# A GRU, two attentions and a mixture of experts on one core: gate inputs formed inside the GRU loop, weights loaded a stage ahead, a filter stage in overlapping batches

## The chip, the cores and the metric

One NeuronCore of a Trainium2 chip runs the whole program, in float32. The metric is the device time of one execution in microseconds (us); lower is better.

## The reference

x has 4 batches of 512 tokens of 512 features. The cut reference:

```python
for t in range(512):                       # GRU over the tokens, h starts as cond
    gi = x[:, t] @ W_ih + b_ih;  gh = h @ W_hh + b_hh
    r = sigmoid(gi_r + gh_r);  z = sigmoid(gi_z + gh_z)
    n = tanh(gi_n + r * gh_n);  h = (1 - z) * n + z * h
a = differential_attention(hs)             # 16 heads, causal and reversed, rotary, lambda
a = filter_over_tokens(a)                  # a fixed 512x512 circulant matrix
x1 = x + head_rms_norm(a) * w @ Wout
xn = rms_norm(x1) * (1 + scale(cond)) + shift(cond)
y = full_attention(xn) @ W_out
out = x1 + y + moe(y)                      # 64 experts, top 6, plus a shared expert
```

Each GRU step needs the h of the step ahead. The gate inputs gi need only x.

## The kernel before, in words

The program is a row of stages, each a function with one block per engine (PE, ACT, DVE, POOL, and SP for DMA), with semaphores between the engines and a barrier at its end. Each engine runs its instructions in the order in which they are written. Weights for the next stage are loaded into one buffer, `ahead`, where that is free.

`gate_inputs_stage` (L55) turns x into `xT` with PE transposes, spreads W_ih into `wih`, forms the r and n gate inputs of all 512 tokens (`gates`, L110 to L125: 4 batches, 8 tiles of 128 gate columns, 4 matmuls each of 512 tokens), moves them with bias into `giT` (L142 on ACT, L144 on DVE), and forms the z inputs as rows in `giz` (L132).

`gru_stage` (L195) loads W_hh on three queues (`load`, L234), then runs 512 steps. One step on PE: `add_z_input` (L292, waits for `pick_ready`, since a small matrix `pick` selects the step's row out of `zin`), `add_bias` (L287), then three gates of 16 matmuls (`gate`, L300) into PSUM tiles pr, pn and pz. The first gate waits for `h_ready`, in halves of h. DVE transposes the rows, ACT forms the sigmoids and tanh, and two DVE scans per step make h, one for each half (`HALVES`, L228, L393); then DVE copies h into `hsT`, which lies in the tile `wide` (L400). POOL copies a block of 32 steps of z inputs into `zin` (L275) and then one `pick` for each step (L280), two buffers deep. The PE and DVE loops hold two steps for each round.

`diff_attention_stage` (L408) follows, loading h and weights per group through SP. `filter_stage` starts with SP loads of filt, wout, wemb, and small vectors, among them a transposed load of cond (L1030), forms scale and shift with 64 matmuls (L1048), and then runs a loop over 4 batches, each in a straight line: filter matmuls (L1055), squares on ACT, head norms on DVE (L1131 to L1140), transposes (L1062), Wout matmuls (L1068), residual and norm, transposes (L1074), xnT. `full_attention_stage`, `route_stage` and `expert_stage` each load their first weights once they have begun; `combine_stage` gathers the expert outputs.

Of the kernel before, what the change touches and what calls it, by code (L numbers as in the profile page):

```python
# [54 lines left out]
def gate_inputs_stage(nc, t, x, W_ih, b_ih, b_hh):  # L55


    with ExitStack() as ctx:
        sem = ctx.enter_context(Sems(nc, "gi_"))
        wih = ctx.enter_context(nc.sbuf_tensor("wih", [P, KD, G3], F32))  # L60
        wraw = t.ahead[:, 0:2 * G3].rearrange("p (a n) -> p a n", a=2)
        xin = ctx.enter_context(nc.sbuf_tensor("gi_xin", [P, 2, TT, D], F32))
        xT = t.wide[:].rearrange("p (b k t) -> p b k t", b=B, k=KD)
        bias = ctx.enter_context(nc.sbuf_tensor("gi_bias", [P, 2, GC], F32))
# [13 lines left out]
        @block.sync  # L78
        def _(sp):
            sp.dma_start(t.ident[:], t.const["ident"]).then_inc(ident_in, 16)  # L80
            for b in range(B):
                if b >= 2:
                    sp.wait_ge(xT_psum, (b - 1) * KD)
                sp.dma_start(xin[:, b % 2, :, :], x[b, :, :].rearrange("(tt p) d -> p tt d", p=P)).then_inc(x_in[b % 2], 16)
            for n, bvec in enumerate((b_ih, b_hh)):
                sp.dma_start(zbias[:, n, :], bvec[D:2 * D].unsqueeze(0).broadcast_to([P, D])).then_inc(zb_in, 16)

        @block.gpsimd
        def _(pool):
            for k in range(KD):  # L90
                if k >= 2:
                    pool.wait_ge(w_spread, 3 * (k - 1))
                pool.dma_start(wraw[:, k % 2, :], W_ih[k * P:(k + 1) * P, :]).then_inc(w_in[k % 2], 16)

        @block.tensor
        def _(pe):
            pe.wait_ge(ident_in, 16)
            for b in range(B):
                pe.wait_ge(x_in[b % 2], 16 * (b // 2 + 1))
                for k in range(KD):  # L100
                    n = b * KD + k
                    if n >= 2:
                        pe.wait_ge(xT_ready, n - 1)
                    for tt in range(TT):
                        last = nc.tensor.transpose(pt[:, k % 2, tt * P:(tt + 1) * P], xin[:, b % 2, tt, k * P:(k + 1) * P], t.ident[:])
                    last.then_inc(xT_psum, 1)
            pe.wait_ge(w_spread, 3 * KD)
            pe.wait_ge(xT_ready, B * KD)

            def gates(b):  # L110
                for c in range(NG):

                    if c >= 4:
                        pe.wait_ge(gi_even if c % 2 == 0 else gi_odd, b * (NG // 2) + (c - 4) // 2 + 1)
                    col = GATES[c // KD] * D + (c % KD) * P
                    for k in range(KD):
                        last = nc.tensor.matmul(pg[:, c % 4, :], wih[:, k, col:col + P],
                                                xT[:, bass.ds(b, 1), k, :].rearrange("p o t -> p (o t)"),
                                                start=(k == 0), stop=(k == KD - 1))
                    last.then_inc(gi_psum, 1)  # L120

                pe.wait_ge(gi_even, b * (NG // 2) + NG // 2)
                pe.wait_ge(gi_odd, b * (NG // 2) + NG // 2)

            with pe.Fori(0, B) as b:  # L125
                gates(b)
            for kb in range(T // 32):
                if kb >= 4:
                    pe.wait_ge(z_out, kb - 3)
                for k in range(KD):  # L130
                    for b in range(B):
                        last = nc.tensor.matmul(pg[32 * b:32 * b + 32, kb % 4, :], xT[:, b, k, 32 * kb:32 * kb + 32], wih[:, k, D:2 * D],  # L132
                                                start=(k == 0), stop=(k == KD - 1))
                last.then_inc(z_psum, 1)

        def evict(eng, b, c, out_sem):

            eng.wait_ge(gi_psum, b * NG + c + 1)
            dst = t.giT[:, :, bass.ds(b + c * B, 1)].rearrange("p t o -> p (t o)")
            g = GATES[c // KD] * KD + c % KD  # L140
            if c % 2 == 0:
                nc.scalar.activation(dst, pg[:, c % 4, :], ACT.Identity, bias=bias[:, 0, g:g + 1]).then_inc(out_sem, 1)  # L142
            else:
                nc.vector.tensor_scalar(dst, pg[:, c % 4, :], bias[:, 0, g:g + 1], None, ALU.add).then_inc(out_sem, 1)  # L144

        @block.scalar
        def _(act):
            for n, bvec in enumerate((b_ih, b_hh)):
                for j in range(KD):
                    for g in GATES:  # L150
                        act.dma_start(bias[32 * j:32 * j + 32, n, g * KD:(g + 1) * KD],
# [3 lines left out]
            with act.Fori(0, B) as b:  # L155
                for c in range(0, NG, 2):
                    evict(act, b, c, gi_even)

# [1970 lines left out]
```

## Time and profile before

| what | us |
|---|---|
| median of 3 runs | 4526.82 (4515.19 to 4535.55) |
| the profiled execution | 4517.86 |
| its span | 4516.1 |
| PE busy | 3734.1 (83%) |
| DVE busy | 2242.8 (50%) |
| ACT busy | 1318.2 (29%) |
| POOL busy | 527.0 (12%) |
| mean granted TensorE clock | 0.945 |

The busy times are shares of the span of one profiled execution. PE is TensorE, PEld its weight loads, which overlap. A float32 matmul appears as two records. A granted clock of 1.00 is 2.4 GHz and 0.50 is 1.2 GHz. A line number such as L305 is a line of the kernel above.

### The profile page before, as it was taken

To read this page: it belongs to the slowest core of one execution; us is meant where nothing else is said; L and a number is where in the kernel's file an instruction comes from. 1 tells how busy PE (TensorE), PEld (TensorE's weight loads), DVE (VectorE), ACT (ScalarE), POOL (GpSimd) and SP (SyncE) were. 2 spreads that over 40 slices of the span, in tenths; PEclk is the share of its full clock that TensorE was granted. 3 is DMA by queue.
4 is the path that set the end of the run, shared out by engine and by line. 5 is a ranking of instruction groups with operands and counts; after the bars stand their busy time and mean duration, and the time that the engine had idled before them with its cause. 6 is when DMAs were issued, how large, how long until landed. Compare 5 with 4: busy or idle time off the path is not lost. (4 is left out here: it accounts for less than half of the span.)

```text
span 4516.1 us, 167227 instructions
## 1 busy us (share of the span) xinstructions
PE 3734.1 (83%) x68303; PEld 2458.8 (54%) x68364; DVE 2242.8 (50%) x6299; ACT 1318.2 (29%) x4238; POOL 527.0 (12%) x1085
## 2 busy tenths in 40 slices
PE   7888888888888888887899998477999979688850
PEld 3277777777777777776444443243333334344420
DVE  2155555555555555554677777133666643222224
ACT  1023333333333333332344444122444411011100
POOL 0000000000000000000222232000000004300026
PEclk9999999999999999999999999688999979899975
DMA  2150000000000000001111110201111111288769
GB/s 70 29 177 0 0 0 0 0 0 0 0 0 0 0 0 0 0 0 39 42 42 49 49 33 17 81 25 50 49 65 49 49 65 57 74 261 261 261 181 202
DMA packets 144489, 256.71 MB, mean 57 GB/s; under 512 B 25943, under 2 KB 76247, under 8 KB 142388
## 3 DMA queue, kind: packets, MB, share of 16 engines
q1 hardware_dynamic: 102004, 159.95, 10.8%
q0 software_dynamic: 21248, 53.30, 4.4%
q10 hardware_dynamic: 21184, 42.76, 3.1%
q8 instruction: 33, 0.54, 0.1%
q14 instruction: 20, 0.16, 0.0%
HBM read 147.89 MB, written 62.92 MB: 47 GB/s over the span
## 5 line engine op out<-in xcount | busy, mean ns | idle before, releaser
L305 PE MATMUL gru_pr<-gru_whh,h 128*4 128x128 f32 x16384 | 543.7, 273 | 230.6 <-DVE h L396 230.6
L305 PEld LDWEIGHTS gru_pr<-gru_whh,h 128*4 128x4 f32 x16384 | 388.4, 87 | 373.9 <-DVE h L396 367.8
L305 PE MATMUL gru_pz<-gru_whh,h 128*4 128x128 f32 x16384 | 541.3, 273 | 1.3 <-issue 1.3
L305 PE MATMUL gru_pn<-gru_whh,h 128*32 128x128 f32 x16384 | 541.7, 273 | 0.0
L305 PEld LDWEIGHTS gru_pn<-gru_whh,h 128*32 128x32 f32 x16384 | 458.4, 110 | 1.3
L305 PEld LDWEIGHTS gru_pz<-gru_whh,h 128*4 128x4 f32 x16384 | 438.3, 87 | 9.3 <-issue 1.4
L376 DVE STREAM_TRANSPOSE gru_tr<-gru_pr 128x128 f32<-128x128 f32 x512 | 162.3, 317 | 380.0 <-PE gru_pr L305 380.0
L340 ACT ACTIVATE gru_rn<-gru_pre 128x16 f32<-128x16 f32 x512 | 118.4, 231 | 700.4 <-DVE gru_pre L378 700.4
L280 POOL COPY gru_pick<-ident 128x4 f32 x512 | 96.5, 188 | 1685.2 <-PE gru_pz L296 1679.9
L891 DVE TENSOR_REDUCE da_mx<-da_ps 128x2 f32<-128x1024 f32 (+3 forms) x256 | 201.2, 817 | 133.5 <-PE da_ps L582 133.5
L389 DVE STREAM_TRANSPOSE gru_tz<-gru_pz 128x64 f32<-128x64 f32 x1024 | 194.6, 229 | 120.2 <-PE gru_pz L305 120.2
L798 ACT ACTIVATE da_probT<-da_ps 128x1024 f32<-128x1024 f32 (+3 forms) x256 | 169.5, 701 | 196.1 <-PE da_ps L603 196.1
L396 DVE TENSOR_TENSOR_SCAN h<-gru_d 128x32 f32<-128x32 f32 x1024 | 185.7, 223 | 78.3 <-ACT gru_d L345 77.8
L296 PE MATMUL gru_pz<-gru_zin,gru_pick 128*4 128x128 f32 x4096 | 205.9, 273 | 19.4 <-DMA gru_whh<-in_L_cond_W_hh 19.4
L380 DVE STREAM_TRANSPOSE gru_tn<-gru_pn 128x128 f32<-128x128 f32 x512 | 162.2, 317 | 119.6 <-PE gru_pn L305 119.6
L342 ACT ACTIVATE gru_d<-gru_narg 128x32 f32<-128x32 f32 x512 | 120.6, 236 | 329.6 <-DVE gru_narg L385 329.6
L345 ACT ACTIVATE gru_d<-gru_tz 128x8 f32<-128x8 f32 x1024 | 176.9, 216 | 128.0 <-DVE gru_tz L389 128.0
L1674 POOL DMA_INDIRECT xg<-ro_yb,ro_slot x96 | 94.4, 983 | 991.7 <-issue 918.5
L290 PE MATMUL gru_pn<-gru_bias,gru_one 128*32 128x128 f32 x4096 | 205.9, 273 | 0.0
L509 POOL TENSOR_SCALAR_AFFINE_SELECT da_probT<-da_probT 128x256 f32<-128x256 f32 x256 | 142.8, 569 | 420.9 <-ACT da_probT L798 420.8
L1864 PE MATMUL ex_pg<-ex_wg,ex_xT 128*128 128x384 f32 x512 | 189.4, 516 | 0.0
L1455 DVE TENSOR_REDUCE fa_mx<-fa_ps 128x2 f32<-128x1024 f32 x128 | 150.5, 1217 | 51.7 <-PE fa_ps L1275 51.6
(266 smaller groups left out, 5457.4 us busy)
## 6 DMA issues: line engine op xcount, KB each, us to landing
ex_wg<-in_L_ffn_gate_up_proj SPq DMA_DIRECT2D x64, 768.0 KB, 4.7
ex_wd<-in_L_ffn_down_proj ACTq DMA_DIRECT2D x64, 384.0 KB, 6.7
xg<-gru_zeros SPq DMA_DIRECT2D x4, 4096.0 KB
da_hb<-wide SPq DMA_DIRECT2D x16, 1024.0 KB, 4.7
fa_hb<-xnT SPq DMA_DIRECT2D x16, 1024.0 KB
ex_xg<-xg ACTq DMA_DIRECT2D x64, 256.0 KB, 6.0
eo<-ex_eo POOLq DMA_DIRECT2D x64, 256.0 KB, 5.4
da_wg<-ahead SPq DMA_DIRECT2D x48, 256.0 KB, 4.9
```

The source lines that it names most:

```text
L290: nc.tensor.matmul(pn[32 * j:32 * j + 32, 0:P], one[:], bias[:, j, :], start=True, stop=False)
L296: last = nc.tensor.matmul(pz[32 * j:32 * j + B, par, 0:P], pick[:, par, :], zin[:, j * P:(j + 1) * P], start=True, stop=False)
L305: last = nc.tensor.matmul(rows(j), of(c), whh[:, c, g, j, :], start=(c == 0 and start), stop=(c == KD - 1))
L345: nc.scalar.activation(cb(d1[:, half * HS:(half + 1) * HS, 2]), tz[:, half * HC:(half + 1) * HC, 0:B], ACT.Sigmoid).then_inc(z_act, 1)
L376: nc.vector.transpose(tr[:].rearrange("p c x -> p (c x)"), pr[:, 0:P]).then_inc(tr_done, 1)
L380: nc.vector.transpose(tn[:], pn[:, 0:P]).then_inc(tn_done, 1)
L389: nc.vector.transpose(tz[:, half * HC:(half + 1) * HC, :].rearrange("p c x -> p (c x)"), pz[:, par, half * 64:(half + 1) * 64]).then_inc(t ...
L396: nc.vector.tensor_tensor_scan(t.h[:].rearrange("p c x -> p (c x)")[:, half * 64:(half + 1) * 64:2], d0[:, of, :].rearrange("p c o -> p (c ...
L798: nc.scalar.activation(probT[:, n % 2, 2 * part:2 * part + 2, n * P:T], ps[:, KBANK[2 * part]:KBANK[2 * part] + 2, n * P:T], ACT.Exp, scal ...
L891: nc.vector.tensor_reduce(mx[:, i, a, 2 * part:2 * part + 2], ps[:, bank:bank + 2, 0:(i + 1) * P], AX, ALU.max).then_inc(max_done, 1)
L1455: nc.vector.tensor_reduce(mx[:, i, 2 * half:2 * half + 2], ps[:, 2 * half:2 * half + 2, :], AX, ALU.max).then_inc(max_done, 1)
L1864: last = nc.tensor.matmul(pg[:, u % 2, 0:2 * I], xT[:, u % 2, k, :], wg[:, u, k, :], start=(k == 0), stop=(k == KD - 1))
```

## The change

1. **Gate inputs.** `gate_inputs_stage` forms the r and n inputs of the first 32 steps only. The others are formed inside the GRU loop, for the block of 32 steps ahead: 8 tiles c, of 4 matmuls k each, one matmul in each step (`next_gate_input`). POOL copies the weights of tile c to a fixed place `wst`, because the loop variable c selects them; DVE moves the finished tile into `giT` after every fourth step (`move_gate_input`). The PE, DVE and POOL loops become 15 blocks of 8 groups of 4 steps, and a last block of 32 steps without gate inputs.
2. **GRU tail.** The two parts of h are one chunk and three (`PARTS`), where they were two and two.
3. **Weights a stage ahead.** A second buffer `ahead2`. W_hh and cond are loaded in the gate input stage, filt in the first attention, the first route weights at the end of the second attention, the gate_up weights of the first 4 experts at the end of the route stage.
4. **Filter.** cond and the small vectors are loaded as rows and turned on PE; scale and shift come from 8 wide matmuls; the batches are unrolled and overlap: PE applies the filter of batch i, then turns y of i - 1 and xn of i - 2, then multiplies by Wout for i - 1.

The core of the diff (semaphore declarations, renamed tiles and the body of DVE's step left out):

```diff
@@ gate_inputs_stage @@
-            with pe.Fori(0, B) as b:
-                gates(b)
+            for c in range(NG):
+                if c >= 2:
+                    pe.wait_ge(gi_out, c - 1)
+                for k in range(KD):
+                    last = nc.tensor.matmul(pg[:, c % 2, 0:B * 32], wih[:, k, c * P:(c + 1) * P], xT[:, k, :, 0:32], start=(k == 0), stop=(k == KD - 1))
+                last.then_inc(gi_psum, 1)
...
+            sp.wait_ge(w_spread, 3 * KD)
+            whh = t.ahead[:].rearrange("p (c g j f) -> p c g j f", c=KD, g=3, j=KD)
+            for jj in range(KD):
+                rows = W_hh.rearrange("(jj c i) n -> jj i c n", jj=KD, c=KD)[jj]
+                for c in range(KD):
+                    sp.dma_start(whh[32 * jj:32 * jj + 32, c, :, :, :].rearrange("i g j f -> i (g j f)"), rows[:, c, :]).then_inc(whh_in, 16)
@@ gru_stage @@
-        HALVES = (0, 1)
-        HC, HS = KD // 2, ST // 2
+        PARTS = (slice(0, 1), slice(1, KD))
...
+            with pool.Fori(0, NBL - 1) as kb:
+                block_of_z(kb)
+                with pool.Fori(0, NG) as c:
+                    pool.wait_ge(gi_out, kb * NG + c + 1)
+                    nc.gpsimd.tensor_copy(wst[:], wih[:, :, bass.ds(c * P, P)]).then_inc(wst_ready, 1)
+                    for k in range(KD):
+                        pick_step(kb, c * KD + k, k)
...
-                    if s is not None and c % HC == 0:
-                        pe.wait_ge(h_ready, s * 2 + (c // HC + 1))
+                    if s is not None and c < 2:
+                        pe.wait_ge(h_ready, s * 2 + (c + 1))
...
-            with pe.Fori(0, T // 2) as q:
+            def next_gate_input(kb, c, k):
+                if k == 0:
+                    pe.wait_ge(gi_out, kb * NG + c + 1)
+                    pe.wait_ge(wst_ready, kb * NG + c + 1)
+                last = nc.tensor.matmul(pgi[:, 0:P], wst[:, k, :], xT[:, k, :, bass.ds(kb * 32 + 32, 32)],
+                                        start=(k == 0), stop=(k == KD - 1))
+                if k == KD - 1:
+                    last.then_inc(gi_psum, 1)
+
+            with pe.Fori(0, NBL - 1) as kb:
+                with pe.Fori(0, NG) as c:
+                    for k in range(KD):
+                        s = kb * 32 + c * KD + k
+                        add_z_input(s, k % 2)
+                        add_bias(s)
+                        next_gate_input(kb, c, k)
+                        step(s, k % 2)
...
+            def move_gate_input(kb, c):
+                dve.wait_ge(gi_psum, kb * NG + c + 1)
+                nc.vector.tensor_tensor(t.giT[:, bass.ds(kb * 32 + 32, 32), bass.ds(c * B, B)], pgi[:, 0:P].rearrange("p (b t) -> p t b", b=B),
+                                        t.gi_bias[:, 0, bass.ds(c, 1)].unsqueeze(2).broadcast_to([P, 32, B]), ALU.add).then_inc(gi_out, 1)
+
+            with dve.Fori(0, NBL - 1) as kb:
+                with dve.Fori(0, NG) as c:
+                    for k in range(KD):
+                        if k == 0:
+                            dve.wait_ge(gi_out, kb * NG + 1)
+                        step(kb * 32 + c * KD + k, k % 2)
+                    move_gate_input(kb, c)
@@ diff_attention_stage, before its first loads of h @@
+            sp.dma_start(t.filt[:], t.const["filt"].rearrange("(s p) t -> p s t", p=P)).then_inc(filt_in, 16)
@@ filter_stage, PE after its first two batches' filters @@
+            for i in range(2, B + 1):
+                if i < B:
+                    apply_filter(i)
+                turn(y[:, (i - 1) % 2, :, :], y_ready, i - 1)
+                moved = tuple(used)
+                turn(xn, normed, i - 2)
+                times_wout(i - 1, moved)
+            turn(xn, normed, B - 1)
@@ full_attention_stage, after its last loads @@
+            sp.dma_start(t.ro_wout, w_out.rearrange("(k p) n -> p k n", p=P)).then_inc(ahead_in, 16)
+            sp.dma_start(t.ro_stage[0:E, 0, :], gate_w).then_inc(ahead_in, 16)
+            sp.dma_start(t.ro_stage[:, 1:4, :], sg_w.rearrange("(c p) n -> p c n", p=P)).then_inc(ahead_in, 16)
@@ route_stage, after its last load @@
+            for u in range(t.EU):
+                sp.dma_start(t.ex_wg[:, u, :, :], gate_up[u].rearrange("(p k) i -> p k i", p=P)).then_inc(S["wg_in"], 16)
```

DVE sets gi_out to 1 ahead of its loop, so the first group waits for nothing.

The order of the instructions at three places of the GRU loop follows. Semaphores are used again by later stages and are printed under the name of their first use: gi_x_in1 stands for gi_out here, gi_xT_ready for z_added, gi_whh_in for zin_ready, gi_w_in0 for wst_ready, gi_xT_psum for pick_ready, gi_x_in0 for the loop's gi_psum, gi_z_out for tn_done, and gi_ident_in for h_ready. A DVE scan is printed as SCALAR_TENSOR_TENSOR. In the kernel before, the same names gi_xT_ready and gi_bias_ready stand for zin_ready and z_added. ISA and REGISTER_ALU rows are waits and address work.

POOL in the block loop of the kernel before, from the copy of a block of z inputs to the end of the loop over steps:

```order
L275 COPY gru_zin<-giz 128x512
L276 UNCONDITIONAL_BRANCH
L276 ISA
L279 ISA [waits gi_xT_ready]
L280 ISA [waits gi_bias_ready]
L280 COPY gru_pick<-ident 128x4
L279 REGISTER_ALU [waits gi_xT_ready]
L280 ISA [waits gi_bias_ready]
L280 COPY gru_pick<-ident 128x4
L276 REGISTER_ALU
L276 COMPARE_AND_BRANCH
```

The same place in the changed kernel, up to the second of a group's four picks:

```order
L262 COPY gru_zin<-giz 128x512
L271 UNCONDITIONAL_BRANCH
L271 ISA
L273 ISA [waits gi_x_in1]
L273 COPY gru_wst<-ahead 128x512
L265 REGISTER_ALU
L266 ISA [waits gi_whh_in]
L267 ISA [waits gi_xT_ready]
L267 COPY gru_pick<-ident 128x4
L266 ISA [waits gi_whh_in]
L267 ISA [waits gi_xT_ready]
L267 COPY gru_pick<-ident 128x4
```

A copy of 128x512 with a wait for gi_out now stands ahead of each group's first pick.

DVE in the changed kernel, from the scans of the fourth step of a group to the end of the inner loop:

```order
L407 SCALAR_TENSOR_TENSOR h<-gru_d 128x16 [waits gru_z_act]
L405 REGISTER_ALU
L407 SCALAR_TENSOR_TENSOR h<-gru_d 128x48 [waits gru_z_act]
L410 REGISTER_ALU
L411 ISA [waits gi_ident_in]
L411 COPY wide<-h 128x16
L414 ISA
L415 ISA [waits gi_x_in0]
L415 TENSOR_TENSOR giT<-gru_pgi,gi_bias 128x32x4
L419 REGISTER_ALU
```

The move of a tile into giT stands behind the scans and the copy of h of the fourth step.

PE in the changed kernel, from the top of a group of four steps to its first gates:

```order
L292 ISA [waits gi_xT_psum]
L294 MATMUL gru_pz<-gru_zin,gru_pick 4x128 [waits gru_tz_done]
L294 MATMUL gru_pz<-gru_zin,gru_pick 4x128 x3
L288 MATMUL gru_pn<-gru_bias,gru_one 32x128 [waits gi_z_out]
L288 MATMUL gru_pn<-gru_bias,gru_one 32x128 x3
L315 ISA
L317 ISA [waits gi_w_in0,gi_x_in1]
L317 MATMUL gru_pgi<-wide,gru_wst 128x128
L301 REGISTER_ALU
L303 MATMUL gru_pr<-ahead,h 4x128 [waits gi_ident_in]
```

The matmul for the block ahead, with its waits in the first step of a group, stands between the bias and the gru_pr gate, which it didn't do before.

## Rows read from the trace of the kernel before

**Rows 1.** Busy time by stretch: length, PE, PEld, DVE, ACT, POOL, clock, DMA, GB/s
```profile
32.00:152.00 120.00, 112.84 (x260) 49.14 (x264) 17.80 (x17) 23.43 (x20) 0.00 (x0) 0.98 0.00 0
152.00:207.00 55.00, 55.00 (x512) 17.55 (x507) 10.38 (x15) 0.00 (x0) 0.00 (x0) 1.00 0.01 1
207.00:226.40 19.40, 0.00 (x1) 0.00 (x1) 3.83 (x14) 1.53 (x3) 3.45 (x8) 0.57 0.83 163
226.40:2122.40 1896.00, 1663.04 (x57344) 1498.29 (x57344) 1038.27 (x4607) 595.03 (x3071) 105.28 (x525) 1.00 0.03 11
...
2836.50:2891.70 55.20, 13.81 (x64) 13.72 (x64) 0.72 (x4) 1.30 (x2) 0.00 (x0) 0.50 0.47 157
2891.70:3084.40 192.70, 148.31 (x384) 74.78 (x384) 65.39 (x124) 39.33 (x104) 0.00 (x0) 0.85 0.05 16
...
3922.80:4366.00 443.20, 352.29 (x1152) 195.97 (x1152) 87.98 (x192) 60.71 (x129) 34.80 (x64) 0.94 0.76 246
```
**Rows 2.** Timeline of one GRU step: start, length, engine, line, [idle before <-releaser]
```profile
1000.53 1.06 PE L305 MATMUL gru_pz<-gru_whh,h 128*4 128x128 f32 x32
...
1001.40 0.40 PE L296 MATMUL gru_pz<-gru_zin,gru_pick 128*4 128x128 f32 x8
...
1001.62 0.40 PE L290 MATMUL gru_pn<-gru_bias,gru_one 128*32 128x128 f32 x8
1001.65 0.38 DVE L389 STREAM_TRANSPOSE gru_tz<-gru_pz 128x64 f32<-128x64 f32 x2 [0.23 <-PE gru_pz L305]
...
1002.00 0.19 POOL L280 COPY gru_pick<-ident 128x4 f32 x1 [3.50 <-PE gru_pz L296]
1002.19 0.36 DVE L396 TENSOR_TENSOR_SCAN h<-gru_d 128x32 f32<-128x32 f32 x2 [0.15 <-ACT gru_d L345]
...
1002.47 1.06 PE L305 MATMUL gru_pr<-gru_whh,h 128*4 128x128 f32 x32 [0.44 <-DVE h L396]
...
1002.67 0.18 DVE L400 COPY wide<-h 128x16 f32 x1
...
1003.34 1.06 PE L305 MATMUL gru_pn<-gru_whh,h 128*32 128x128 f32 x32
```
**Rows 3.** Timeline of POOL at the start of a block of 32 steps
```profile
344.03 0.61 POOL L275 COPY gru_zin<-giz 128x512 f32 x1 [7.19 <-PE gru_pz L296]
344.94 0.41 POOL L280 COPY gru_pick<-ident 128x4 f32 x2 [0.30 <-POOL gru_zin L275]
```
**Rows 4.** Groups of instructions: busy us, mean ns of one, idle before and releaser
```profile
L563 PE MATMUL da_ps<-da_wg,da_hb 128*128 128x128 f32 x512 | 65.3, 281 | 0.0
...
L144 DVE TENSOR_SCALAR giT<-gi_pg,gi_bias 128x512 f32 x16 | 17.5, 1093 | 101.7 <-PE gi_pg L117 101.7
L192 DVE TENSOR_TENSOR giz<-gi_pg,gi_zbias 128x512 f32<-128x512 f32 x16 | 11.1, 692 | 45.2 <-PE gi_pg L132 45.2
```
**Rows 5.** Stretches of the expert stage: length, PE busy, clock, DMA, GB/s
```profile
3992.35:3994.77 2.42, 0.00 (x1) 1.00 0.60 157
3994.77:3998.77 4.00, 4.00 (x11) 0.57 0.97 338
3959.38:3962.04 2.66, 0.00 (x1) 1.00 0.72 203
3962.04:3966.04 4.00, 4.00 (x16) 1.00 0.88 306
```
**Rows 6.** Timeline of PE in the first two GRU steps
```profile
227.21 1.93 PE L305 MATMUL gru_pr<-gru_whh,h 128*4 128x128 f32 x32
...
230.42 1.05 PE L305 MATMUL gru_pz<-gru_whh,h 128*4 128x128 f32 x32
...
236.08 0.62 PE L305 MATMUL gru_pz<-gru_whh,h 128*4 128x128 f32 x15 [1.26 <-issue]
```
**Rows 7.** Timeline at the entry of the filter stage
```profile
2839.84 29.97 SPq L1030 DMA_DIRECT2D fi_condT<-in_cond  x4
...
2876.94 13.81 PE L1048 MATMUL fi_pf<-fi_condT,fi_wemb 128*128 128x4 f32 x64 [41.06 <-DMA fi_bg<-in_L_cond_g_norm]
```
**Rows 8.** Timeline at the entry of the route stage
```profile
3662.76 0.69 PE L1577 MATMUL ro_pa<-ident,ro_stage 64*128 64x64 f32 x4 [16.11 <-DMA ro_sdraw<-in_L_ffn_shared_down_w]
```

More of the change, by code:

```diff
@@ L97, in _ @@
             pe.wait_ge(ident_in, 16)
             for b in range(B):
-                pe.wait_ge(x_in[b % 2], 16 * (b // 2 + 1))
                 for k in range(KD):
[L101 to L106, printed above, removed]
+                    transpose_x(b, k)
@@ L1044, in _, with bank @@
         def _(pe):
[L1045 to L1052 removed]
+            used = [0, 0]
+            def bank(v):
+                if used[v]:
+                    pe.wait_ge(dve_moved if v else act_moved, used[v])
+                used[v] += 1
+                return pt[:, v, :]
@@ new lines, in _ @@
+            pe.wait_ge(cond_ready, 2)
+            to = bank(1)
+            for k in range(KD):
+                for n in range(2):
+                    last = nc.tensor.matmul(to[32 * n:32 * n + B, :], condT[:, k, :], wemb[:, k, n * D:(n + 1) * D],
+                                            start=(k == 0), stop=(k == KD - 1))
+            last.then_inc(turned, 1)
+            turn(y[:, 0, :, :], y_ready, 0)
+            moved = tuple(used)
+            pe.wait_ge(emb_ready, 2)
+            to = bank(1)
@@ new lines, in _ @@
+            for k in range(KD):
+                last = nc.tensor.transpose(to[:, k * NR:(k + 1) * NR], embr[:, k * P:(k + 1) * P], t.ident[0:NR, 0:NR])
+            last.then_inc(turned, 1)
+            pe.wait_ge(wout_in, 16)
+            times_wout(0, moved)
+            for i in range(2, B + 1):
+                if i < B:
+                    apply_filter(i)
+                turn(y[:, (i - 1) % 2, :, :], y_ready, i - 1)
+                moved = tuple(used)
+                turn(xn, normed, i - 2)
+                times_wout(i - 1, moved)
@@ new lines, in _ @@
+            dve.wait_ge(cond_ready, 2)
+            dve.sem_inc(dve_moved, 1)
+            norm_heads(1)
+            dve.wait_ge(turned, 2)
+            dve.wait_ge(embr_zero, 1)
+            for n in range(2):
+                nc.vector.tensor_copy(embr[32 * n:32 * n + B, :], pt[32 * n:32 * n + B, 1, :]).then_inc(emb_ready, 1)
+            dve.wait_ge(emb_ready, 2)
+            dve.sem_inc(dve_moved, 1)
+            seen[0] += 2
+            keep_y(0)
+            seen[0] += 1
+            dve.wait_ge(turned, seen[0])
@@ L1521, in _, with route_stage @@
             output(NIT - 1)
-def route_stage(nc, t, W_out, gate_w, sg_w, su_w, sd_w):
+def route_stage(nc, t, su_w, sd_w, gate_up):
     with ExitStack() as ctx:
```

533 lines of the change are left out of this document (284 added, 249 removed).

## The prediction

> **What bounds the kernel now.** I read the busy times by stretch first, then the timeline of one GRU step, then the same step's neighbours on POOL, then the places where the change touches other stages. The stretches [rows 1] show that 1,896 of the 4,516 us are the 512 GRU steps, at a TensorE clock of 1.00 (2.4 GHz), 3.70 us each. Inside a step PE idles 0.44 us ahead of the gru_pr gate, released by DVE's scan that makes h [rows 2]: the loop is a recurrence PE, DVE, ACT, DVE, PE, and whatever is put between that scan and the next gru_pr gate lengthens it. What PE does in the gap (z input from 1001.40, bias from 1001.62, so 0.22 us of issue) is hidden. Ahead of the loop lie 120 us of gate inputs, 55 us of z inputs and 19.4 us of waiting for W_hh [rows 1]. The filter stage waits 55 us at its entry, and its own 192.7 us hold only 148.3 us of PE at a clock of 0.85 [rows 1].
>
> **The change part by part**, summed against the profiled execution (4517.9 us; the median of the runs shown, 4526.8, is 9 us above it). About 0.5%, 23 us, is what a measurement of this kernel can tell from no change.
>
> (a) Gate inputs ahead of the GRU. Removed from the stage: 256 records of 0.43 us of issue, the 120 us. Left: block 0 only, 8 tiles x 4 matmuls, two records each, at 0.128 us a record (65.3 us / 512 for 128x128 in [rows 4]), 8 us, plus a cold start, 9 us. The 55 us of z inputs stay. Gain 111. W_hh is now loaded under the z inputs; of the 19.4 us there remain DVE's memsets (3.8 us busy in [rows 1]) and one small load, 5.5 us. Gain 14. Together **-125**. The order of the x and W_ih loads differs, but the bytes are the same: bounds -115 and -130.
>
> (b) Filter stage. Its entry wait of 41 us is for small loads, among them the transposed cond load that SP takes 30 us to issue, and 13.8 us of matmuls follow [rows 7]. Both go: the filter is preloaded, and these matmuls become 8 wide ones between batches: 54 us. The body: PE's 148.3 us at 0.85 are 126 at full clock, plus 5 for the cond work. Of 44 us of idle time I keep about 25: the last head norms and the last root still stand ahead of a turned batch in about five places, some 4 us each, with a tail at the end. That is 156 in place of 193. Together **-91**, bounds -75 and -100.
>
> (c) Route stage: its first matmul comes at 3662.76, after 16.1 us of idle time for loads [rows 8]. W_out, gate_w and sg_w are now there; sd_w and su_w (1.5 MB) are still waited for a little later: **-8**, bounds 0 and -11. (d) Expert stage: it runs at 246 GB/s with DMA busy 0.76 [rows 1], so 3 MB of weights fetched earlier are worth 3 / 0.246 = 12 us: **-11**, bounds 0 and -14. (e) The attention stage's first h load now stands behind the 1 MB filter load on SP's queue, 4 us at that rate: **+3**, bounds 0 and +5.
>
> (f) Uneven tail. Two transposes take 0.38 us, two scans 0.36, and the first scan's end releases PE 0.06 us later [rows 2]. A first part of one chunk frees PE up to 0.08 us sooner, but after 4 matmuls (0.22 us) PE waits for the second part, whose transpose and scan are now three chunks long. They end about when the second halves did. I take 0.01 us a step, **-5**; bounds -40 (0.08 x 512) and +10.
>
> (g) What the GRU loop gains. Per step one matmul, 0.26 us, and its address work go into the 0.44 us gap: nothing in three steps of four; if it didn't fit, 0.1 us x 360 = 36 us, which the range holds. The fourth is another matter. In the order of DVE, move_gate_input stands behind the whole fourth step. Its signal gi_out releases two things: POOL's copy of the next weights (wst), which stands ahead of the four picks on POOL, and PE's first matmul of the next group. PE's z input of step 4c+4 needs the first pick. So once in four steps this chain lies between the scan and gru_pr. From the end of the second scan (1002.19 + 0.36 = 1002.55) by the rows: the h copy ends at +0.30 (1002.67 + 0.18) [rows 2]. The move is 128 elements out of PSUM into giT. Of 512 elements such an operation takes 0.69 us, into strided giT 1.09 [rows 4], so it lies between 0.17 and 0.55; I take 0.35, nearer a quarter plus fixed cost, and 0.05 of dispatch: +0.70. POOL starts 0.20 after its release (1001.80 to 1002.00 [rows 2]); the wst copy has the size of the zin copy, 0.61 us, and after that one the pick started 0.30 later where it waited for it; picks in a row follow each other by about 0.22 [rows 3]. Pick done at +1.75 (to 2.0). PE starts z at +1.85, then 0.22, 0.22, 0.26 for the gate input and 0.15 for waits and addresses: gru_pr at +2.70. Now it starts at -0.08. The stall is **2.8 us**, bounds 2.2 and 3.5. It occurs for c = 1 to 7 of 15 blocks and for c = 0 of 14: 119 times, **+333**, bounds +262 and +417.
>
> (h) The clock. In this stall PE idles from the end of gru_pz (1000.53 + 1.06, or -0.96) to +1.85, 2.8 us. No GRU step shows such a gap. The nearest rows are in the expert stage: after 2.42 us of idle the clock was 0.57 over the next 4 us, after 2.66 us it stayed at 1.00 [rows 5]; of the eight gaps of 1.9 to 2.7 us at full clock in this trace (these are two) six were followed by a fall to 1.2 GHz, for some 3.4 us. The price of cold gates: the first step of all, after 19 us of idle, took 3.21 us for its first two gates (227.21 to 230.42), where a warm gate takes 0.87 (1002.47 to 1003.34), so 1.5 us a fall [rows 2, 6]. With a fall in three of four stalls: 1.1 us, **+131**. Bounds 0 (it never falls) and 3 us a stall, +357 (two such stretches).
>
> Sum: 4517.9 - 125 - 91 - 8 - 11 + 3 - 5 + 333 + 131 = 4746; with the 9 us of the median, **4755 us**, 5% slower.
>
> **The rivals.** (1) *Faster.* The gains are 237 us; the hand-over decides at 237 / 119 = 1.99 us. If DVE's move, POOL's copy and the picks overlap more than the rows show (a copy of 0.3 us, a pick right behind it) and the clock holds, a stall of 1.7 us gives 4526.8 - 237 + 202 = 4492. For it: waits that are long satisfied cost little here. Against: four operations on three engines in strict order, each with a row. 0.07. (2) *No difference,* the same with 1.9 to 2.1 us: 0.03. (3) *The clock holds*: 4755 - 131 = 4624. For it: two gaps of eight; GRU steps keep 1.00 with their own short gaps. 0.22. (4) *The clock falls long*: another 1.8 us a stall, 4755 + 214 = 4969. For it: the filter stage, with 44 us of gaps in 193, ran at a mean clock of 0.85 [rows 1]. 0.13. (5) *Code loading.* PE's loop body doubles to four steps. At the second step ever, PE stood 1.26 us for nothing but issue [rows 6]. Were that paid each time round the longer body, 120 x 1.26 = 151 us more: 4906. Against: it is not paid again in the two-step loop, where each gap ends with DVE. 0.05. The Trainium skill (Runtime: NRT & Kernel Launch, "Instruction fetch mechanics") says that a taken branch whose target is outside the window held forces a fetch and a stall, while it gives PE room for 2048 instructions. Some 230 matmuls of four instructions each would be inside that, by that page; no run here shows the count.
>
> **How the numbers follow.** The forecast has 0.50, the rivals 0.50. The range reaches from rival 3 with a stall of 2.6 us (4624 - 24 = 4600) to just under rival 4, **4600 to 4950**; that leaves out rivals 1 and 2 and half of rival 4. Faster 0.07, within 0.5% 0.03, slower 0.90.
>
> **What would show it.** In the profile after: the GRU loop begins near 102 us and takes about 2,355 us. On POOL one 0.6 us copy in every four steps, released by DVE's move into giT; PE's z matmul then waits for POOL's pick, 119 times about 2.8 us. The granted clock of the loop is about 0.90. The filter stage takes about 157 us with no entry wait, the experts about 432. The forecast is wrong if PE's waits for the pick are under 1 us, or if the loop's clock is 1.00; if the GRU loop still takes under 2,130 us, the change wins.

## The result, and the profile of the changed kernel

| | before | changed |
|---|---|---|
| median of 4 runs | 4525.65 us | 4800.05 us |
| lowest and highest | 4515.19, 4535.55 | 4775.56, 4810.63 |
| span of the profiled execution | 4516.1 us | 4809.0 us |
| mean granted clock | 0.945 | 0.921 |

The ratio is 1.060, with a 95% interval of 1.055 to 1.065. The change makes the kernel 6% slower, against 5% (4755 us) forecast.

I read the stretches first, cut where TensorE (PE) starts and ends a stage. Busy time by stretch, changed kernel (columns as in [rows 1]):

```profile
33.70:42.30 8.60, 7.65 (x68) 7.37 (x72) 0.56 (x1) 3.74 (x8) 0.00 (x0) 1.00 1.03 211
42.30:97.40 55.10, 55.06 (x512) 16.46 (x512) 10.36 (x15) 0.37 (x1) 0.00 (x0) 1.00 0.02 4
97.40:103.90 6.50, 0.04 (x4) 0.05 (x8) 3.83 (x14) 1.62 (x3) 1.95 (x5) 0.83 0.44 164
103.90:2491.30 2387.40, 2029.11 (x58304) 1691.51 (x58304) 1113.99 (x4723) 612.72 (x3068) 163.60 (x644) 0.92 0.02 8
2491.30:3209.00 717.70, 647.42 (x5011) 286.27 (x5068) 492.80 (x639) 322.94 (x516) 183.54 (x288) 0.96 0.14 44
3209.00:3389.20 180.20, 143.28 (x410) 70.03 (x409) 66.17 (x124) 40.56 (x106) 0.00 (x0) 0.89 0.17 60
...
3954.40:4218.10 263.70, 215.02 (x704) 108.51 (x704) 96.27 (x229) 32.22 (x78) 94.09 (x96) 0.94 0.18 63
4218.10:4648.60 430.50, 360.78 (x1152) 202.78 (x1152) 87.96 (x192) 60.02 (x128) 34.11 (x63) 0.92 0.77 245
```

Ahead of the GRU the plan works: the gate inputs take 8.6 us, not 120, the wait for W_hh has become 6.5 us, and the first GRU matmul starts at 103.9 us, not 226.4. The loop behind it loses four times as much. Its 2,387.4 us, at a clock of 0.92, stand against the 1,894.9 us, at 1.00, that the same cut gives for the kernel before:

```profile
226.40:2121.30 1894.90, 1663.02 (x57344) 1498.29 (x57344) 1037.53 (x4603) 594.57 (x3069) 105.28 (x525) 1.00 0.03 11
2835.90:3081.90 246.00, 162.08 (x448) 88.50 (x448) 65.30 (x127) 41.11 (x106) 0.00 (x0) 0.78 0.14 48
3646.70:3922.80 276.10, 216.99 (x704) 109.42 (x704) 96.75 (x229) 32.23 (x78) 94.40 (x96) 0.91 0.16 55
3922.80:4357.00 434.20, 352.28 (x1152) 195.97 (x1152) 87.98 (x192) 60.11 (x128) 34.25 (x63) 0.94 0.77 250
```

What PE waits for in the changed kernel's loop says which term it is. Waits of PE from 103.9 to 2491.3 us (line, releaser: us in total, times, longest):

```profile
PE gru_pz L294 <- POOL gru_pick L267: 342.0, 120, 6.5
PE gru_pr L303 <- DVE h L407: 14.0, 46, 0.4
PE gru_pz L303 <- issue: 4.7, 2, 3.5
PE gru_pn L288 <- issue: 4.0, 1, 4.0
```

The first row is 6.5 us ahead of the loop and 119 waits of 2.82 us in it. The wait for DVE's scan, which the matmul of the next gate input now fills, is all but gone. One hand-over, once in four steps, in the timeline of the changed kernel:

```profile
1010.36 1.06 PE L303 MATMUL gru_pz<-ahead,h 128*4 128x128 f32 x32
...
1011.98 0.44 DVE L407 TENSOR_TENSOR_SCAN h<-gru_d 128x16 f32<-128x16 f32 x2
1012.54 0.18 DVE L411 COPY wide<-h 128x16 f32 x1
1012.90 0.29 DVE L415 TENSOR_TENSOR giT<-gru_pgi,gi_bias 128x128 f32 x1 [0.17 <-issue]
1013.36 0.61 POOL L273 COPY gru_wst<-ahead 128x512 f32 x1 [4.85 <-DVE giT L415]
...
1013.91 0.32 POOL L267 COPY gru_pick<-ident 128x4 f32 x2
1014.24 0.40 PE L294 MATMUL gru_pz<-gru_zin,gru_pick 128*4 128x128 f32 x8 [2.82 <-POOL gru_pick L267]
1014.45 0.40 PE L288 MATMUL gru_pn<-gru_bias,gru_one 128*32 128x128 f32 x8
1014.79 0.49 PE L317 MATMUL gru_pgi<-wide,gru_wst 128*128 x2
...
1015.20 1.06 PE L303 MATMUL gru_pr<-ahead,h 128*4 128x128 f32 x32
```

The scans end at 1012.42, gru_pr starts 2.78 us later. What is to be seen is a file of five operations on three engines, one behind the other: DVE's h copy, DVE's move, POOL's copy, POOL's pick, PE's z input.

What that wait does to the clock stands in the four hand-overs that follow one another here, each with the same wait of 2.82 us. First PE's timeline, then the busy time of the 4 us behind each:

```profile
1014.24 0.40 PE L294 MATMUL gru_pz<-gru_zin,gru_pick 128*4 128x128 f32 x8 [2.82 <-POOL gru_pick L267]
...
1031.76 0.40 PE L294 MATMUL gru_pz<-gru_zin,gru_pick 128*4 128x128 f32 x8 [2.82 <-POOL gru_pick L267]
...
1068.46 0.61 PE L294 MATMUL gru_pz<-gru_zin,gru_pick 128*4 128x128 f32 x8 [2.82 <-POOL gru_pick L267]
...
1088.80 0.61 PE L294 MATMUL gru_pz<-gru_zin,gru_pick 128*4 128x128 f32 x8 [2.82 <-POOL gru_pick L267]
```

```profile
1014.24:1018.24 4.00, 4.00 (x130) 3.58 (x130) 1.26 (x6) 0.47 (x2) 0.19 (x1) 1.00 0.00 0
1031.76:1035.76 4.00, 4.00 (x130) 3.58 (x130) 1.26 (x6) 0.47 (x2) 0.19 (x1) 1.00 0.00 0
1049.28:1053.28 4.00, 4.00 (x82) 3.49 (x86) 0.49 (x2) 0.23 (x1) 0.19 (x1) 0.67 0.00 0
1068.46:1072.46 4.00, 4.00 (x62) 2.79 (x66) 0.32 (x1) 0.00 (x0) 0.19 (x1) 0.50 0.00 0
```

In the same 4 us PE gets through 130 records at 2.4 GHz and 62 at 1.2 GHz. From hand-over to hand-over a group takes 17.5 us with the clock held (1014.24 to 1031.76), 19.2 with a short fall (1049.28 to 1068.46), and 20.3 to 20.8 with a long one (1068.46 to 1088.80). Over the loop's 118 groups, 57 hold the clock and 61 do not. It is no accident of the run: one pattern repeats every 16 groups, 8 held and 8 fallen (three short, five long).

### The profile page after: what moved, and what is told of

Its sections match the earlier page's. It is cut to its first block and busy times, and to the rows that moved or that the text cites. A ratio compares the mean times of both kernels' runs of the same rounds, so it can differ in the third digit from the quotient of the medians.

```text
span 4809.0 us, 169712 instructions
## 1 busy us (share of the span) xinstructions
PE 3982.5 (83%) x69032; PEld 2596.8 (54%) x69093; DVE 2302.2 (48%) x6400; ACT 1316.6 (27%) x4227; POOL 584.6 (12%) x1201
## 5 line engine op out<-in xcount | busy, mean ns | idle before, releaser
L303 PE MATMUL gru_pr<-ahead,h 128*4 128x128 f32 x16384 | 600.6, 289 | 14.0 <-DVE h L407 14.0
L303 PE MATMUL gru_pn<-ahead,h 128*32 128x128 f32 x16384 | 597.5, 291 | 0.0
L303 PE MATMUL gru_pz<-ahead,h 128*4 128x128 f32 x16384 | 572.5, 283 | 4.7 <-issue 4.7
L303 PEld LDWEIGHTS gru_pn<-ahead,h 128*32 128x32 f32 x16384 | 503.3, 118 | 10.6
L303 PEld LDWEIGHTS gru_pz<-ahead,h 128*4 128x4 f32 x16384 | 455.9, 91 | 33.5 <-issue 5.3
L303 PEld LDWEIGHTS gru_pr<-ahead,h 128*4 128x4 f32 x16384 | 366.3, 91 | 164.9 <-DVE h L407 29.8
L400 DVE STREAM_TRANSPOSE gru_tz<-gru_pz 128x32 f32<-128x32 f32 (+1 forms) x1024 | 194.8, 228 | 151.7 <-PE gru_pz L303 151.7
L407 DVE TENSOR_TENSOR_SCAN h<-gru_d 128x16 f32<-128x16 f32 (+1 forms) x1024 | 226.8, 229 | 57.3
L317 PE MATMUL gru_pgi<-wide,gru_wst 128*128 x960 | 247.3, 341 | 0.0
L354 ACT ACTIVATE gru_d<-gru_tz 128x4 f32<-128x4 f32 (+1 forms) x1024 | 198.3, 216 | 142.8 <-DVE gru_tz L400 142.8
```

Of the source, the lines that this page charges most:

```text
L303: last = nc.tensor.matmul(rows(j), of(c), whh[:, c, g, j, :], start=(c == 0 and start), stop=(c == KD - 1))
L317: last = nc.tensor.matmul(pgi[:, 0:P], wst[:, k, :], xT[:, k, :, bass.ds(kb * 32 + 32, 32)], start=(k == 0), stop=(k == KD - 1))
L354: nc.scalar.activation(cb(d1[:, part.start * B:part.stop * B, 2]), tz[:, part, 0:B], ACT.Sigmoid).then_inc(z_act, 1)
L400: nc.vector.transpose(tz[:, part, :].rearrange("p c x -> p (c x)"), pz[:, par, part.start * 32:part.stop * 32]).then_inc(tz_done, 1)
L407: nc.vector.tensor_tensor_scan(t.h[:].rearrange("p c x -> p (c x)")[:, part.start * 32:part.stop * 32:2], d0[:, of, :].rearrange("p c o -> ...
```

## The experiments

Four questions were open: whether the wait is the order of the work or the work itself (e1); what of the loss is the wait and what the clock (e4); how the wait divides (e2, e3); and why the small terms came out as they did (e5 to e9). e1 to e4 ran on one chip, e5 and e6 on a second, e7 to e9 on a third; the kernel before took 4517.9, 4541.7 and 4527.4 us there, so kernels on different chips are compared by their ratio to it. e2, e3 and e4 rest on two runs each, the others on four to six.

### e1: DVE's move one step earlier

```diff
                     for k in range(KD):
                         if k == 0:
                             dve.wait_ge(gi_out, kb * NG + 1)
+                        if k == KD - 1:
+                            move_gate_input(kb, c)
                         step(kb * 32 + c * KD + k, k % 2)
-                    move_gate_input(kb, c)
```

> The changed kernel with one call moved: DVE's move of the gate inputs stands ahead of the fourth step of a group, where DVE waits 0.65 us for the gru_pr gate, and no longer behind it. Theory (the stall is the order of DVE's move): the move, POOL's copy of 0.61 us and the picks all come a step earlier, PE never waits for a pick, the granted clock of the loop is 1.00, a group of four steps takes 4 x 3.64 = 14.6 us in place of 17.5 (clock held) or 20.4 (clock fallen), the GRU loop 1,870 us in place of 2,387, the kernel about 4,295 us (4,280 to 4,320), 5% under the kernel before. Rival (the longer loop body, loaded code, or the added matmul itself costs): a group stays over 15.5 us and the kernel over 4,400 us with an issue gap in each group. Rival (POOL is the bound: a copy of 0.61 us does not fit into a step): PE still waits for the pick, about 0.6 us a group, 4,370 us.

Measured: 4301.7 us, 0.953 of the kernel before (0.951 to 0.955), and 498 us under the changed kernel (483 by the two ratios). PE's waits from 110 to 1900 us hold no row of POOL's pick. A group in its timeline:

```profile
1005.05 0.19 DVE L411 COPY wide<-h 128x16 f32 x1
1005.40 0.29 DVE L415 TENSOR_TENSOR giT<-gru_pgi,gi_bias 128x128 f32 x1 [0.17 <-issue]
...
1005.86 0.61 POOL L273 COPY gru_wst<-ahead 128x512 f32 x1 [8.63 <-DVE giT L415]
...
1006.41 0.32 POOL L267 COPY gru_pick<-ident 128x4 f32 x2
...
1007.39 0.40 PE L294 MATMUL gru_pz<-gru_zin,gru_pick 128*4 128x128 f32 x8
```

The same instructions with the same durations: the move stands where DVE would wait for gru_pr anyway, POOL has its picks ready by 1006.73, and PE asks for one at 1007.39. The steps follow each other by 3.64 us and the clock of the loop is 1.00. So these 480 to 500 us are the place of one instruction in DVE's order. The rival of a longer loop body falls: PE has three issue gaps of over 1 us in the loop, 9.0 us in all; two lie in its first 20 us and one at the last block's own loop, and none comes again.

### e4: the wait kept, PE busy in it

```diff
                         s = kb * 32 + c * KD + k
+                        if k == 0:
+                            for _ in range(3):
+                                nc.tensor.matmul(spare[:], whh[:, 0, 0, 0, :], bias[:].rearrange("p j f -> p (j f)"), start=True, stop=True)
                         add_z_input(s, k % 2)
```

> The changed kernel with three matmuls of 128x512 that compute nothing (into a PSUM bank that nobody reads) ahead of the wait for the first pick of a group; they take 3 x 0.86 = 2.6 of the 2.8 us in which PE idles. Theory (two costs: the stall, and the falls of the clock that the idle time brings): the stall stays, the clock of the loop is 1.00, every group takes 17.5 us (57 of 118 do now, the others 19.2 to 20.8), the loop loses 118 x 1.31 = 155 us, and the kernel takes about 4,645 us. Rival (the clock falls for another reason, such as the matmuls' own load): no change, 4,800 us, or slower. Rival (the filler delays the z input): a group takes over 17.8 us.

Measured: 4651.5 us, 1.031 of the kernel before (1.028 to 1.033), 149 us less than the changed kernel (133 by the ratios) for 360 useless matmuls more: three ahead of each of the 120 groups, 119 of which have the wait. Timeline of PE, then the loop's busy time:

```profile
1011.71 2.84 PE L329 MATMUL gru_spare<-gru_bias,ahead 128*128 128x512 f32 x6
...
1014.60 0.40 PE L295 MATMUL gru_pz<-gru_zin,gru_pick 128*4 128x128 f32 x8
...
1015.15 0.49 PE L318 MATMUL gru_pgi<-wide,gru_wst 128*128 x2
```

```profile
103.10:2339.00 2235.90, 2207.60 (x59024) 1731.01 (x59024) 1116.50 (x4731) 614.14 (x3070) 163.80 (x647) 1.00 0.03 9
```

The clock is 1.00 and the next filler starts at 1029.22, 17.5 us after this one. This parts the two costs: the loops of changed kernel and e4 differ by 2387.4 - 2235.9 = 151.5 us, which is the clock; e4's and e7's (1888.7, below) by 347.2 us, which is the wait, 2.92 us each of 119 times. e4's stretch begins with its first filler, 4.4 us ahead of its first z input, so each of the two is known to about 5 us; a plain group of 17.51 us in e4 against 14.55 in e7 gives 2.96.

### e2 and e3: how the wait divides

e2 puts the first pick ahead of POOL's copy:

```diff
+                    pick_step(kb, c * KD, 0)
                     pool.wait_ge(gi_out, kb * NG + c + 1)
                     nc.gpsimd.tensor_copy(wst[:], wih[:, :, bass.ds(c * P, P)]).then_inc(wst_ready, 1)
-                    for k in range(KD):
-                        pick_step(kb, c * KD + k, k)
+                    for k in range(1, KD):
+                        pick_step(kb, c * KD + k, k % 2)
```

e3 lets POOL copy the next weights when PE has read the last ones, not when DVE has moved their result (gi_psum starts one higher there, and its other waits are one higher with it):

```diff
-                    pool.wait_ge(gi_out, kb * NG + c + 1)
+                    pool.wait_ge(gi_psum, kb * NG + c + 1)
                     nc.gpsimd.tensor_copy(wst[:], wih[:, :, bass.ds(c * P, P)]).then_inc(wst_ready, 1)
```

> The changed kernel with the first pick of a group ahead of POOL's copy of the weights; DVE's move stays where it is. Theory (a chain of DVE's move, POOL's copy, PE's matmul): z input and bias are issued in their normal place, PE's gate input matmul waits for the copy, which ends 0.94 + 0.61 us after the scan; gru_pr starts at +2.0 in place of +2.8, so a group at full clock takes 16.7 us in place of 17.5. PE idles some 1.9 us in place of 2.8. If the clock falls as often, the kernel takes about 4,705 us; if it holds, 4,550. Rival (the pick and z input are the stall): the wait vanishes, a group takes 14.6 us, 4,300 us.

> The changed kernel with POOL's copy of the weights released by PE's last matmul of the tile and no longer by DVE's move. Theory: copy and picks lie a step ahead, and only DVE's move (end at +0.77 us after the scan) stands between the scan and PE's gate input matmul, then 0.26 us for it: gru_pr at about +1.2 us, a stall of 1.3 us, a group of 15.9 us; PE's longest idle time is 1.2 us, and the clock holds at 1.00. Loop 2,030 us, kernel about 4,450 us; 4,530 with as many falls of the clock at half the price. Rival (POOL's 0.61 us copy is nothing, DVE's move is the whole stall): still 17.5 us a group, 4,800 us.

Measured: e2 4594.2 us, ratio 1.018 (1.015 to 1.021); e3 4483.4 us, ratio 0.993 (0.991 to 0.996). The loops' busy time and PE's longest wait in them, e2 and then e3:

```profile
103.90:2281.80 2177.90, 1878.63 (x58304) 1609.26 (x58304) 1115.37 (x4724) 614.50 (x3070) 163.75 (x646) 0.99 0.03 9
...
PE gru_pgi L318 <- POOL gru_wst L274: 272.8, 119, 2.4
```

```profile
105.20:2166.30 2061.10, 1867.52 (x58304) 1607.35 (x58304) 1155.57 (x4723) 614.16 (x3068) 163.13 (x644) 1.00 0.03 9
...
PE gru_pgi L317 <- DVE giT L416: 167.9, 119, 1.5
```

A group at full clock takes 16.94 us in e2 (16.7 expected) and 16.05 in e3 (15.9), against 17.51. So the chain has the links that the prediction gave it, and taking one out shortens it by that link. Against e7's loop, e3 costs 172.4 / 119 = 1.45 us a group; that is DVE's share. e2 costs 289.2 us, of which 12 are falls of the clock: 2.33 us, so POOL's copy adds 0.88, and the pick, z input and bias behind it the remaining 0.59 of 2.92.

Read together the runs also rank the idle times: after 2.82 us in the changed kernel 61 of 118 groups had a fallen clock, after 2.29 us in e2 8 of 118, after 1.41 us in e3 none. The last 0.5 us of the wait were the dear ones: e2 takes 70 us off it and 139 off the clock. The groups of the three kernels differ in length too (17.5, 16.9 and 16.1 us), and no run changes the wait alone, so this is a ranking of three cases and not a threshold. The Trainium skill (TensorE: Matmul & The Clock Gate, Part 1) says that the window over which the chip judges TensorE's activity is free-running and doesn't reset when a kernel starts. The pattern of 16 groups with one and the same wait fits that, and no run here shows the window itself.

### e5: the uneven tail alone

```diff
-        HALVES = (0, 1)
-        HC, HS = KD // 2, ST // 2
+        PARTS = (slice(0, 1), slice(1, KD))
```

The loops over the halves in the kernel before become loops over the parts, as in the change; nothing else is touched.

> The kernel before with the uneven tail alone: the last transposes, sigmoids and scans of a step work on one chunk and then on three, in place of two and two. The prediction's term (f): 0.01 us a step, 5 us, so 0.999 of the kernel before. Theory from the traces of the changed kernels, whose steps without a hand-over are 3.64 us apart against 3.69 before, with one matmul more: the first part frees PE 0.05 us earlier and the second is not waited for, 512 x 0.05 = 26 us less, 0.994 of the kernel before, and 3.63 to 3.64 us from gru_pr to gru_pr. Rival (the shorter steps come from another part, such as the weights read from another buffer or the code's layout): 3.69 us a step and 1.000.

Measured: 4515.9 us against 4541.7, 0.993 (0.991 to 0.996), 26 us. PE's timeline of the kernel before, and of e5:

```profile
503.60 1.06 PE L305 MATMUL gru_pr<-gru_whh,h 128*4 128x128 f32 x32 [0.45 <-DVE h L396]
507.29 1.06 PE L305 MATMUL gru_pr<-gru_whh,h 128*4 128x128 f32 x32 [0.44 <-DVE h L396]
```

```profile
503.19 1.09 PE L304 MATMUL gru_pr<-gru_whh,h 128*4 128x128 f32 x32 [0.37 <-DVE h L394]
506.82 1.08 PE L304 MATMUL gru_pr<-gru_whh,h 128*4 128x128 f32 x32 [0.37 <-DVE h L394]
```

3.69 us a step become 3.63 to 3.64, and PE's wait 0.37 in place of 0.44. The first part saves 0.07 us there, the second gives 0.02 back, since gru_pr's 32 matmuls now last 1.09 in place of 1.06.

### e6: the RMS weight in few pieces

The filter stage takes 180.2 us, 23 more than forecast, and 18.3 of them are one wait. Timeline of the changed kernel: SP's issue, DVE, PE:

```profile
3211.89 0.40 SPq L1063 DMA_DIRECT2D fi_rmsw<-in_L_attn_rms_weight  x1
...
3242.49 0.43 DVE L1252 TENSOR_SCALAR fi_rmsw<-fi_rmsw 128x512 f32<-128x512 f32 x1 [31.27 <-DMA fi_rmsw<-in_L_attn_rms_weight]
...
3245.29 15.72 PE L1088 MATMUL fi_pf<-A,ahead 128*128 128x512 f32 x32 [18.30 <-DVE fi_y L1221]
```

The load writes the same 32 numbers 16 times into each of 128 partitions. e6 is e1 with:

```diff
-            sp.dma_start(rmsw[:].rearrange("p o (h d) -> p (o h) d", h=H), rms_row.broadcast_to([P, H, DH])).then_inc(rms_in, 16)
+            sp.dma_start(rms1[:], rms_weight.unsqueeze(0).broadcast_to([P, DH])).then_inc(rms_in, 16)
...
-            nc.vector.tensor_scalar(rmsw[:], rmsw[:], 1.0 - LAMBDA_INIT, None, ALU.mult).then_inc(rms_ready, 1)
+            nc.vector.tensor_scalar(rmsw[:].rearrange("p o (h d) -> p (o h) d", h=H), rms1[:].unsqueeze(1).broadcast_to([P, H, DH]),
+                                    1.0 - LAMBDA_INIT, None, ALU.mult).then_inc(rms_ready, 1)
```

> The changed kernel with DVE's move ahead of the fourth step (as in e1_move_early), and in the filter stage the RMS weight loaded as one row of 32 numbers per partition (128 pieces) and spread over the heads by the DVE instruction that scales it, in place of a load that repeats it 16 times in each partition (2,048 pieces of 128 bytes, landed 30 us after its issue). Theory: PE's wait of 18.3 us for DVE at the filter stage's second batch goes, to at most 2 us; the stage takes 163 to 165 us in place of 180, and the kernel 4,285 us in place of 4,302. Rival (the 6 to 15 us that SP needs to issue the next loads, or their bytes, delay whatever stands ahead of them, small or not): the weight still lands late, and the kernel stays at 4,300.

Measured: 4302.0 us, 0.946 of the kernel before (0.943 to 0.949). In its timeline the load is there 2.9 us after its issue and PE does not wait:

```profile
2713.80 0.35 SPq L1064 DMA_DIRECT2D fi_rms<-in_L_attn_rms_weight  x1
...
2716.74 0.43 DVE L1253 TENSOR_SCALAR fi_rmsw<-fi_rms 128x512 f32<-128x512 f32 x1 [3.62 <-DMA fi_rms<-in_L_attn_rms_weight]
```

```profile
2710.90:2870.90 160.00, 141.66 (x410) 69.30 (x409) 66.44 (x124) 40.55 (x106) 0.00 (x0) 0.93 0.18 66
...
3436.60:3734.20 297.60, 232.91 (x704) 122.16 (x704) 95.90 (x229) 32.81 (x79) 93.91 (x96) 0.86 0.18 60
```

The filter stage takes 160.0 us in place of 179.9 (e1). But the second row, the route stage up to the first expert, took 297.6 us where e1's (3461.0 to 3737.6) took 276.6, at a clock of 0.86 against 0.89, so this profiled execution is only 5 us shorter than e1's.

Two more numbers say what the wide load did. In the changed kernel, while it was under way (3212.3 to 3241.3), the DMA engines were busy for 0.08 of the time and moved 21 GB/s; in the 14.8 us from 3242.5 they moved 409. So neither its 256 KB nor the traffic of other loads explains its 30 us. And SP needed 5.99 and 14.78 us to issue the two large loads behind it, where it needs 0.43 and 0.50 in e6. The rival of e6 had the order the wrong way round: the small pieces held up SP and the large loads. The Trainium skill (DMA: Bandwidth & Descriptors, "Why small descriptors are slow") puts a fixed overhead on every packet of a transfer to or from device memory; the rows agree in kind, 30.6 us until use for 2,048 pieces of 128 bytes and 2.9 us for 128 of them; how much of it is that overhead no run here shows, as e6 has a sixteenth of the bytes too.

### e7 and e8: is the filter stage's gain kept?

e7 is e1's kernel again, e8 is e6's, on one chip.

> The kernel of e1_move_early once more, for a comparison on one chip with the next two. Expected: 0.953 of the kernel before, as in its first run.

> The kernel of e6_rms_narrow once more, beside e7_move_early_again on one chip. In its trace the filter stage was 20 us shorter, and the route stage behind it 21 us longer at a granted clock of 0.86 in place of 0.89. Theory (the time saved stays: the route stage's clock varies from run to run and has nothing to do with the filter stage): 20 us, 0.4%, under e7_move_early_again, with a route stage of about 277 us in this trace. Rival (the clock takes it back: less idle time ahead is paid with falls later): a route stage near 297 us again, and no difference between the two kernels.

Measured: e7 4306.9 us (4293.3 to 4318.6), ratio 0.953; e8 4283.5 us (4275.0 to 4293.0), ratio 0.948 (0.945 to 0.950). The 23 us stay. e7's loop is the one that the differences above are taken against:

```profile
105.50:1994.20 1888.70, 1861.42 (x58304) 1593.48 (x58304) 1115.15 (x4723) 614.48 (x3068) 164.43 (x645) 1.00 0.03 10
```

The route stage itself, from its first matmul to POOL's last instruction, took 256.2 us in e8's trace, 250.1 in e7's, 256.4 in e1's and 277.4 in e6's (3440.4 to 3717.8), at clocks of 0.92, 0.95, 0.92 and 0.89, with the same work each time. e6 and e8 are one kernel and lie 21 us apart there. Up to the first expert e8 took 277.0 us (3438.8 to 3715.8), as the theory has it; it is 6 us over e7, not the 20 that the rival wants. What makes the clock fall in this stage stays open.

### e9: the first experts' weights not ahead

In route_stage the four loads into t.ex_wg and their wait go, in expert_stage they come back, and PE's wait for them too:

```diff
-            for u in range(t.EU):
-                sp.dma_start(t.ex_wg[:, u, :, :], gate_up[u].rearrange("(p k) i -> p k i", p=P)).then_inc(S["wg_in"], 16)
-            sp.wait_ge(S["wg_in"], 16 * t.EU)
...
+            for u in range(U):
+                load_gate_up(sp, u, u)
```

> The kernel of e7_move_early_again with the first four experts' gate and up weights (3 MB) loaded in the expert stage again, and not ahead in the route stage. The prediction's term (d): 11 us more. Rival (the expert stage is not bound by those bytes, only its first experts wait for them): 3 to 4 us more at its entry, and no more.

Measured: 4311.7 us (4301.5 to 4314.2), 4.8 us over e7, with overlapping runs. From the stage's start to its first matmul 9.4 us pass, against 5.8 in e7 (3728.87 to 3738.25, 3726.71 to 3732.47), 3.6 us more, as the rival says. But the expert stage with its loads ahead took 410 to 415 us to its last matmul in e1, e7 and e8, and 430.5 in the changed kernel, so 5 and 11 us aren't told apart for certain. The stage of the kernel before varies as much: from its first to its last matmul 425.6 us in that kernel's trace and 410.4 in e5's, which has the same instructions there. It stays open.

## Why the prediction was right, and where its terms were off

By the prediction's own steps, the profiled executions against each other (4809.0 - 4516.1 = 292.9 us):

| step | predicted | measured | from |
|---|---|---|---|
| (a) gate inputs, W_hh | -125 | -122.5 | first GRU matmul at 103.9, before 226.4 |
| (b) filter stage | -91 | -65.8 | 246.0 to 180.2 |
| (c) route stage | -8 | -12.4 | 276.1 to 263.7 |
| (d) expert stage | -11 | -3.7 | 434.2 to 430.5 |
| (e) attention's start | +3 | +3.1 | 714.6 to 717.7 |
| (f) tail, and what the loop gains in plain steps | -5 | -6.2 | loops of e7 and before |
| (g) the stall, 119 times | +333 | +347.2 | loops of e4 and e7 |
| (h) the clock | +131 | +151.5 | loops of the changed kernel and e4 |
| the rest | 0 | +1.7 | |

**(g) held, link by link.** The prediction had gru_pr at +2.70 us from the end of the second scan; it came at +2.78. It had the h copy ending at +0.30 (measured 1012.72, so +0.30), the move at +0.70 (1013.19, +0.77), POOL's pick done at +1.75 (the first of the two between +1.49 and +1.81), z input at +1.85 (1014.24, +1.82). The move, which no row of before showed, took 0.29 us inside its bounds of 0.17 and 0.55. What the sum missed is the plain step that shrank beside it: taken from the loops, the stall is 2.92 us, not 2.8. The dependence was read out of the order of the code, each duration out of a row of a neighbour of the same size, and e1 shows that the order is the cause.

**(h) came out near for a reason only partly right.** The prediction let three of four stalls lose the clock, at 1.5 us. In fact 61 of 118 groups lost it, and the mean price was 151.5 / 61 = 2.5 us, since five of eight falls are long and cost 2.9 us (20.4 in place of 17.5). Two errors of opposite sign gave 1.27 us a stall for 1.1, so that this term came near is partly luck. Its share of three in four came from gaps of 1.9 to 2.7 us in the trace before; that trace has nine of these at full clock with seven falls, not eight with six, and none of them in a loop like this one. e4 shows the mechanism: with PE busy in the same wait no fall is left.

**(b) is the term that failed.** It said of the entry: "Both go: the filter is preloaded". The transposed loads and the 13.8 us of matmuls did go. One load that the change kept, the RMS weight, was hidden behind the longer wait of before and became the next thing late, 18.3 us for PE. SP's timeline of the kernel before, with the load right ahead of the cond load of [rows 7]:

```profile
2838.99 0.81 SPq L1028 DMA_DIRECT2D fi_rmsw<-in_L_attn_rms_weight  x1
```

It landed 34.6 us after this issue, at 2873.6, 3.3 us ahead of PE's first matmul. So the two loads were under way together, and of the 30 us that SP needs to issue cond the prediction put all to cond; how much was the RMS load's isn't shown. With it mended the stage takes 160.0 us, against the 157 forecast, so the body was sized right and the entry was not. It is the question that the prediction put to other steps ("what is late next") and left out here.

**(f) was right in sum and wrong in both parts.** The tail alone saves 26 us (e5), not 5: the first scan on one chunk frees PE 0.07 us sooner, and the second part is there when PE gets to it. The loop gives about 20 us back: 9 us of issue gaps paid once against 1.3 before, and about 0.4 us a block of 32 steps; some 5 us aren't traced. That the one added matmul of a step would fit into PE's gap held.

**(a), (c), (e)** are within 5 us of their terms. For (c) the entry is what changed: PE's wait of 16.1 us is 4.4 in the changed kernel, and the rest of the stage took as long, 235.1 and 234.5 us from its first to its last matmul. The same instructions took 264.2 us in e5's trace, so that the two agree is chance. **(d)** was the gain of 3 MB at the stage's mean rate; e9 points to the entry wait alone, 3.6 us, without settling it, and the -3.7 of the table lies within what the unchanged stage varies by.

**The sum.** The terms on record add up to 227 us and not quite to the 4746 written there (4745, and 4754 with the 9 us). Measured are 292.9: (b) 25 us, (h) 20, (g) 14 and (d) 7 more than forecast, all in one direction. The direction of the change and the two terms that decide it were right, the sizes of the smaller ones less so.

**The rivals.** Rival 1 asked for a hand-over under 1.99 us: e3 with 1.45 us is just that case, and it is indeed faster than before, by 0.7%. Rival 3 (the clock holds) is what e4 makes, forecast at 4624, measured at 4651. Rival 4 lies 169 us off. Rival 5, code loading each time round, is excluded: the groups of the changed kernel with a held clock agree within 0.02 us, and the long issue gaps come once. (A block's last group, always one with a fallen clock here, is 0.3 us longer than the others of its kind.)

## What to carry to other kernels

An operation put into a recurrence's free time is priced by its own duration only on the engine that has the free time. Its hand-overs must be followed through each engine's order: here 0.29 us of DVE work, placed at the end of a step and not in the wait of 0.65 us a step earlier, cost some 490 us. Split a suspected wait with kernels that take one link out each, and keep PE busy in it once, so that what it costs itself and what it costs through the clock stand apart.

When a change removes the wait that ended last, list what else arrives in its shadow: a broadcast of 128-byte pieces, which had landed in time behind a longer wait, took 18 us of the 54 expected.

## What the runs showed that I had not expected

Of the same wait of 2.82 us half the cases lost the clock and half did not, in a pattern that repeats every 16 groups through the loop; of 2.29 us 8 in 118 lost it. A little less idle time was worth far more than its own length.

360 matmuls whose result nobody reads made the kernel some 140 us faster.

The fastest kernel of the study, e8, has all parts of the change, DVE's move one step earlier and the narrow load. It takes 4283.5 us, 5.2% under the kernel before (0.945 to 0.950), and 11% under the change as it was made.
